# Second layer: a block's turn_over and its products in the middle of a turn of attention, five maxima behind them

## The reference

```python
q = split_heads(queries @ Wq.T); k = split_heads(keys @ Wk.T); v = split_heads(values @ Wv.T)
scores = jnp.einsum('bhqd,bhkd->bhqk', q, k) * scale
attn = jax.nn.softmax(scores, axis=-1)
...
x = x + _L1_xattn_ref(_layernorm(x, axis=-1), ctx_1024, ctx_1024, L1_xattn_Wq, ...)
x = x + _L1_ffn_ref(_layernorm(x, axis=-1), L1_ffn_W, L1_ffn_b, L1_ffn_V_r, L1_ffn_C)
```

## Time and profile before

| | |
|---|---|
| median of 3 runs | 856.89 us (855.26 to 858.37) |
| the profiled execution | 856.55 us, its span 854.9 us |
| busy over the span | PE 780.5 us (91%), DVE 476.2 (56%), ACT 263.9 (31%), POOL 280.0 (33%) |
| chain that ended last | PE 70%, DVE 19%, ACT 4%, issue 4%, DMA 1% |
| mean granted TensorE clock | 0.978 of full speed |
| second layer's turns | from about 628 us on |

### The profile page before, as it was taken

How to read it: one execution, slowest core, us unless ns; L and a number is a source line. 1 busy time by engine, 2 the same in 40 slices (tenths; PEclk the granted TensorE clock), 3 DMA queues, 4 the chain that set the end, 5 groups by cost and what they waited for, 6 DMA issues and landing times.

```text
span 854.9 us, 14297 instructions
## 1 busy us (share of the span) xinstructions
PE 780.5 (91%) x5120; PEld 511.2 (60%) x5120; DVE 476.2 (56%) x1100; ACT 263.9 (31%) x524; POOL 280.0 (33%) x298
## 2 busy tenths in 40 slices
PE   6998989999999979989999999999888898898995
PEld 4675557665765545556665666555665566665673
DVE  2548484247444556624434554636667876778633
ACT  1223212321142112112222222231245654464451
POOL 4754415141500412601721526355952311101012
PEclk8999999999999979999999999999999999999998
DMA  9899414431520672735676655675856754733000
GB/s 242 219 303 314 135 51 158 136 99 56 173 92 1 215 272 100 267 110 157 184 211 182 197 149 172 195 206 168 240 144 170 190 156 128 192 94 100 24 24 22
DMA packets 70678, 133.54 MB, mean 156 GB/s; under 512 B 10401, under 2 KB 51362, under 8 KB 68690
## 3 DMA queue, kind: packets, MB, share of 16 engines
q1 hardware_dynamic: 54864, 81.14, 30.7%
q10 hardware_dynamic: 7906, 31.23, 13.3%
q0 software_dynamic: 7840, 20.26, 8.6%
HBM read 104.02 MB, written 28.41 MB: 155 GB/s over the span
## 4 chain that ended last, share of the span: by engine, by line
PE 70%; DVE 19%; ACT 4%; issue 4%; DMA 1%; POOL 0%; SPq 0%; DVEq 0%; POOLq 0%
PE ps L1319 15%; PE ps L1013 10%; DVE mxh L1614 7%; PE ps L1336 7%; PE ps L1024 6%; PE ps L1948 4%; PE ps L1034 4%; PE ps L1941 2%; PE ps L1977 2%; PE ps L956 2%; PE ps L1326 2%; PE ps L1044 2%; PE ps L990 2%; PE ps L1923 2%; PE ps L943 1%
## 5 line engine op out<-in xcount | busy, mean ns | idle before, releaser
L1614 DVE TENSOR_REDUCE mxh<-ps 112x2 f32<-112x750 f32 x128 | 114.9, 933 | 38.2 <-PE ps L1948 37.9
L1319 PE MATMUL ps<-rw,rowsT 128*128 x280 | 128.9, 603 | 1.5 <-ACT rowsT L1280 0.9
L1814 ACT ACTIVATE d_pT<-ps 125x448 f32<-125x448 f32 x192 | 91.0, 549 | 82.8 <-PE ps L1968 79.4
L1013 PE MATMUL ps<-x1T,sw 128*128 128x448 f32 x256 | 102.9, 548 | 10.1 <-DVE gluT L465 8.1
L1319 PEld LDWEIGHTS ps<-rw,rowsT 128*128 128x128 f32 x280 | 50.3, 190 | 57.6 <-issue 57.6
L1013 PEld LDWEIGHTS ps<-x1T,sw 128*128 128x128 f32 x256 | 46.7, 190 | 56.3 <-issue 39.2
L1948 PE MATMUL ps<-kst,qst 96*112 96x375 bf16 x256 | 65.3, 344 | 12.6 <-DVE mxh L1614 8.0
L1336 PE MATMUL ps<-rw,gT 128*128 x280 | 66.4, 380 | 0.8 <-ACT gT L1284 0.8
L1336 PEld LDWEIGHTS ps<-rw,gT 128*128 128x128 f32 x280 | 52.9, 190 | 21.4 <-issue 16.0
L1024 PE MATMUL ps<-sw,gluT 128*112 128x256 f32 x256 | 59.2, 387 | 1.4 <-issue 1.4
L325 POOL DMA_INDIRECT xg<-xh_moe,places x32 | 32.4, 1014 | 85.7 <-DVE places L552 49.0
(11 more groups left out here) (236 smaller groups left out, 1258.8 us busy)
## 6 DMA issues: line engine op xcount, KB each, us to landing
rb<-in_rb SPq DMA_DIRECT2D x35, 512.0 KB
kst<-kscr ACTq DMA_DIRECT2D x45, 378.0 KB, 5.3
rw<-in_rw SPq DMA_DIRECT2D x24, 512.0 KB
kscr<-ka SPq DMA_DIRECT2D x16, 567.0 KB, 3.5
cT<-in_ctx_t SPq DMA_DIRECT2D x21, 378.0 KB, 4.3
ctxT<-in_ctx_t SPq DMA_DIRECT2D x16, 378.0 KB
ctxn<-in_ctx SPq DMA_DIRECT2D x16, 336.0 KB
qst<-qscr ACTq DMA_DIRECT2D x12, 448.0 KB, 7.3
```

What stands on the lines that cost most here:

```text
L1013: last = mm(bank[up_in(i, m)[k]][:, 0:GS], w[:, e, c, h * P:(h + 1) * P], x1T[:, c, :], start=c == 0, stop=c == C - 1)
L1319: last = mm(bank[1 + 2 * q + k], rowsT[:, q, c * P:(c + 1) * P], w[:, e, c, :], start=c == 0, stop=c == C - 1)
L1614: V.tensor_reduce(mxh[:, 2 * g:2 * g + 2], ps[0:S, 2 * (g % 2):2 * (g % 2) + 2, 0:K], axis=AX_X, op=ALU.max).then_inc(s["s_max"], 1)
L1814: A(pT[:, q % 2, k, :], bank[4 + k][0:KC, 0:QUAD * S], ACT.Exp).then_inc(s["p_ready"], 1)
```

## The change

In the turns with a block, except turn 15, turn_over follows outputs_T at once, and score(2) and the rest come behind; the multiplication follows score(2); score(3) waits for the block's copies or additions, and scores 3 to 7 with their maxima stand behind that. TensorE's new order: outputs_T, turn_over, outputs 0, transposed 2, score 2, queries or projection, outputs 1, transposed 3, score 3, score 4, outputs 2, score 5, score 6, score 7. ScalarE copies the turned-over rows behind exps 1 instead of behind exps 2 and the queries behind exps 2 instead of behind exps 3. VectorE adds the block's products behind maximum 2 instead of behind maximum 6. In the turns that have no block, maximum 3 stands behind `normalized` instead of ahead of it; this makes a difference in turns 4, 7 and 11, since in the others nothing is normalized or nothing is left to score. TensorE's order in the turns without a block is as before.

```diff
@@ VectorE
             if ahead_of:
                 maximum(b + 2, 2)
-                maximum(b + 2, 3)
+            if what is not None and b < B - 1:
+
+                if what == "o":
+                    attended(i)
+                elif what == "f":
+                    results(i)
+                if ahead_of:
+                    maximum(b + 2, 3)
             if kind is not None:
                 normalized(v, k, NORMS[kind, k])
             if ahead_of:
+                if what is None:
+                    maximum(b + 2, 3)
                 maximum(b + 2, 4)
                 maximum(b + 2, 5)
                 maximum(b + 2, 6)
-            if what == "o":
-                attended(i)
-            elif what == "f":
+            if b == B - 1:
                 results(i)
@@ ScalarE
             exps(b, 1)
+            if what is not None and b < B - 1:
+                turned_over(what, i)
             if b in (G, 2 * G):
...
                 exps(b, 2)
-                if what is not None:
-                    turned_over(what, i)
+                if what == "q":
+                    for m in range(C):
+                        query_out(a, i, m, bank[2 + m])
             exps(b, 3)
             if b + 4 < B:
                 load_keys(a, b + 4)
-            if what == "q":
-                for m in range(C):
-                    query_out(a, i, m, bank[2 + m])
@@ TensorE
             if b + 1 < B:
                 t.wait_ge(s["mT_ready"], b + 2)
+            if what is not None:
+
+                if what == "o":
+                    t.wait_ge(s["heads_ready"], (i + 1) * G * 2)
+                else:
+                    t.wait_ge(s["xh_ready"], (NORMS[what, i] + 1) * G)
+                turn_over(heads[:, i * G:(i + 1) * G, :] if what == "o" else xh)
+                outputs(b, 0)
+                transposed(b, 2)
+                t.wait_ge(s["T_ready"], TN + TURNS[what, i] * C + C)
+                score(2)
+                t.wait_ge(s["heads_ready"], b * 2)
+                if what == "q":
+                    queries(i)
+                elif what == "o":
+                    project("o", i, wo1, "o_ps")
+                else:
+                    project("f", i, wf, "f_ps")
+                outputs(b, 1)
+                transposed(b, 3)
+                if what == "q":
+                    t.wait_ge(s["q1_ready"], (i + 1) * C)
+                elif what == "o":
+                    t.wait_ge(s["x3_ready"], i * G + G)
+                else:
+                    t.wait_ge(s["res_ready"], i * G + G)
+                score(3)
+                score(4)
+                outputs(b, 2)
+                score(5)
+                score(6)
+                score(7)
+                continue
             score(2)
             outputs(b, 0)
...
```

More of the change, by code:

```diff
@@ L2071, in tensor @@
             outputs(b, 1)
[L2072 to L2079, removed]
             transposed(b, 3)
-            if what is not None:
-                t.wait_ge(s["T_ready"], TN + TURNS[what, i] * C + C)
             score(6)
[L2085 to L2093, removed]
-            outputs(b, 2)
[L2095 to L2100, removed]
+            outputs(b, 2)
             score(7)
```

## The result

| | before | after |
|---|---|---|
| median (4 runs each) | 857.63 us (855.26 to 858.5) | 868.51 us (867.74 to 869.8) |
| ratio | | 1.012, 95% interval 1.0074 to 1.0166 |
| profiled execution, its span | 856.55, 854.9 | 869.8, 868.1 |

What follows compares the result with a forecast made beforehand. Each turn was taken to end with VectorE's maximum 7. Terms of + 2.25, + 0.73, - 3.1, + 5.1 and + 4.3 summed to + 9.3 on 856.55 us, 865.85, or 866.2 adjusted to the median; range 860.4 to 870.0.

Steps and rivals of the forecast that it cites:

- A turn ends with maximum 7: All turns: VectorE's maximum 7 sets the end; what TensorE ends earlier than this buys nothing.
- Block turns with a projection: Turns 6, 8, 10, 12, 13: VectorE sets the end from score(3) on; each longer by 0.45, 2.25 for five.
- Turn 5: The queries' turn: score(3) starts at 7.42, five maxima follow, and the turn gets longer by 0.73.
- Turn 6: Gains 3.1: 1.65 from the collision with GpSimd's split of the queries, 1.44 from the clock; its 0.45 counted with block turns.
- Normalizing turns: Turns 4, 7, 11: maximum 3 behind the normalization, TensorE's score(5) waits; each longer by 1.7 at full clock, 5.1 for three.
- The clock there: Turns 4, 7, 11: TensorE's 2.4 idle brings the lower clock level; 1.44 a fall, 4.3 for three turns.
- Other queues at nothing: SP's stores and row copies, ScalarE's query copies, key loads and last-queries load move in time, all at no cost.
- A: Rival: the clock holds in turns 4, 7 and 11; 861.9 us, chance 0.20.
- B: Rival: the clock falls behind block turns too, 1.44 for each of six turns; 874.8 us, chance 0.07.
- C: Rival: other work between scores stretches the block turns' maxima, 0.8 a turn and more; about 868.3 us, chance 0.10.
- D: Rival: not slower, TensorE's idle time takes back maximum 3's delay in normalizing turns; 856.8 us, chance 0.09.
- E: Rival: faster, D and the tail of the block turns free as well; 853.8 us, chance 0.04.

Runs made afterwards that it cites:

- later split: Kernel before, GpSimd's split of the queries held back until the negated parts ending turn 5, their store put off to turn 7: 849.30 us, ratio 0.9952.
- the wait filled: Changed kernel with 40 unused TensorE multiplications between score(4) and score(5) in turns 4, 7 and 11: 856.25 us, ratio 1.0027.
- the softmax ahead: Changed kernel with outputs(1) and transposed(3) ahead of score(5) on TensorE in turns 4, 7 and 11: 854.72 us, ratio 1.0008.
- maximum 3 alone: Kernel before with only maximum 3 moved behind the normalization in turns 4, 7 and 11, block turns in the old order: 861.60 us, ratio 1.0094.

## Why the prediction was right

- **A turn ends with maximum 7.** Right. In the block turns TensorE has waits of 0.32 behind its block work and the turn's length follows the maxima.
- **Block turns with a projection, + 0.45.** + 0.34 to 0.36 where nothing else changed. Score(3) was put at t = 7.80 and went at 7.82. The term was a little large since five maxima in a row take 4.32, a step of 0.85, and not the 4.41 that I scaled from four.
- **Turn 5, + 0.73.** + 0.56: half of the difference for the same reason, the rest because score(3) went at t = 7.38, not 7.42, and its maximum 0.52 later, not 0.56.
- **Turn 6, - 3.1 + 0.45 = - 2.65.** - 2.55. The collision left 0.26 (0.43 less 0.17) against 0.2 expected, and the clock held. The later split shows on its own that the two terms were 3.3 together (18.21 to 14.91), not how they part.
- **Normalizing turns, + 1.7 at full clock.** 1.71, 1.69 and 1.69 with the wait filled. TensorE's wait was put at 2.4 and was 2.43 in turn 11; normalized did start 1.55 behind the means. The floor that the prediction named, 0.8 a turn if TensorE were no bound behind score(5), is what the run with the softmax ahead measured (0.82 to 0.83). It is the step that the title of the change does not name, and it carries the result: 10.8 us in the first profile with its falls.
- **The clock there, 1.44 for each of three falls.** It fell in nine of nine such turns (the changed kernel twice, maximum 3 alone). The price was mis-sized: against the turns with the wait filled it was 1.5 in six of them, but 2.3 to 2.7 where the spell lasted 6 us and more (turn 7 twice, turn 4 once). In the first profile the three falls cost 5.7 against 4.3 priced. That is 1.4 us more; the block turns and turn 5 took 0.5 of it back.
- **Other queues at nothing.** Nothing in the profile speaks against it.
- **The sum** was + 9.3; by turns it is + 10.2, by the medians + 10.9 and, timed again, + 9.2. The interval of the first ratio spans some 8 us, so that the sum came so near is in part luck; that each term came near is not.
- **The rivals.** A (the clock holds behind 2.4 of idle) never happened. B (falls behind block turns) did not either: six profiles of kernels with the new order in six turns each show none in 36 turns, though TensorE's scores there alternate with maxima through PSUM banks and idle between them. Of the rule that the Trainium skill has on this (page "TensorE: Matmul & The Clock Gate", section "A second HAM failure mode: psum-queue depth-cycling") no block turn here shows an instance: waits of 0.32 between scores did not do it. Clustered waits of 1.7 in sum, in turns 4, 7 and 11 with the old order, sometimes did; whether these falls are of the page's kind the runs do not tell. C (a dearer tail, block turns over 15.7) did not come: they took 15.25 to 15.26. D and E asked for normalizing turns that cost nothing, and these cost 1.7 even at full clock.
- **One reading was too firm.** From the single profile of before I took that a wait of 1.15 leaves the clock alone. Other executions show the fall behind the same wait. At 1.1 us a fall and 4 falls in 12 turns this is about 1 us in the comparison, not the sign.

## What to carry to other kernels

When a diff reorders a list that several branches share, work out each branch, also those that its title does not name; here that one cost nearly all. The reduction that was moved behind a wait for a third engine cost its own time once (0.8 of the 1.7) and, because TensorE's queue held ready work behind the same wait, time for that work too (the other 0.9): look at what is queued behind, and put the ready work ahead. A small instruction on the path that is far longer than its equals (1.40 against 0.17) is worth a look: here holding back the other engine's work gained 0.5%, where the whole reordering lost 1.2%.

## What the runs showed of the hardware

- TensorE's level behind waits of about a microsecond differs from execution to execution of the same instructions. In turns 4, 7 and 11 with the old order (waits 1.15, 0.32, 0.22 close together) it fell in 4 of 12 turns of four profiles, 1.1 us each time; with outputs moved ahead (waits 0.46, 0.32, 1.06 or 1.02) in 2 of 3; with the softmax ahead (waits 1.15 and 1.03 to 1.10, 1.9 us of work between them) in none of 3; with 24 or 40 unused multiplications in the wait in none of 9 (with 40, a wait of 1.26 still followed 1.33 us of them); with a wait of 2.4 to 2.5, and 1.15 ahead of it, in 9 of 9. One profile without a fall is no evidence that the wait is harmless.
- The spell at 1.2 GHz lasted 3 to 4 us as a rule, 6 to 7 us in several cases, 10 in the run with the softmax ahead (630 to 640, ahead of turn 1) and 13 in the first profile of the changed kernel, with TensorE busy nearly all along; I found no reason in the profile for which it is.
- VectorE's small instructions between SBUF tiles ended when GpSimd's instruction ended: tensor_scalar 1.40 and 0.43 in place of 0.17, cast 0.79. Maxima that read PSUM kept 0.93 beside the same instructions. The Trainium skill (page "GPSIMD Engine Reference", section "1. Specifications") says that GpSimd and VectorE share SBUF interfaces and contend where VectorE is in a two-port mode or has two SBUF inputs. The trace does not record the mode, so for tensor_scalar and cast, with one tile as input, it shows the lengthening and not its condition. For two inputs it agrees: in the kernel before, at the start of turn 4 and beside GpSimd's additions (676.12 to 679.27), the next two took 0.60 and 0.62 in place of 0.18:

```profile
676.29 0.60 DVE L1623 SCALAR_TENSOR_TENSOR mr<-mxh,mparts 112x16 f32<-112x16 f32 x1
...
677.13 0.62 DVE L1627 TENSOR_TENSOR mparts<-mr,mparts 112x16 bf16<-112x16 f32 x1
```
